# Moving small pieces of the first round between VectorE, ScalarE and GpSimd, and cutting v's projection in two

## The chip, the cores and the metric
One core of one Trainium2 chip runs the whole kernel. The metric is device time in microseconds, as the median of several executions.

## What is computed
A transformer block with a conditioning vector per sequence, then a conditioned layer norm. x has 64 sequences of 64 tokens of 256 features; there are 16 heads of 16 features, and a hidden layer of 1024.

```python
x = x + a_alpha * attention(gamma_a * rmsnorm(x) + beta_a)      # gamma, beta, alpha: t @ w.T, per sequence
x = x + f_alpha * (silu(h @ gate_w.T) * (h @ hidden_w.T) @ out_w.T + out_b)
#   with h = gamma_f * rmsnorm(x) + beta_f
y = (layernorm(x) * weight + bias + tanh(cond @ lin_w.T + lin_b)) * weight + bias
```

## The kernel before, in words
The 4096 tokens are cut into eight groups of eight sequences (512 tokens). Every stage of a group holds 128 partitions by 512 columns or a multiple. Products in full precision are made of three passes: each fp32 operand is split into a high part, which is the operand rounded to fp32r, and a low part, the rest; TensorE does high by high, low by high and high by low (`passes`). The weights are split this way too, once, during the first round: nine chunks are loaded through stage buffers (`stage`, chunks 0 to 8: wqk, wv, wo, four quarters of gh, two halves of wout), a rounding makes the high part (`cut_hi`) and a subtraction the low part (`cut_lo`).

The order of the work on each engine is written out by hand: each engine has its own queue of instructions, which waits on semaphores. In the loop the attention of group g runs interleaved with the feed-forward part of group g - 1. The first round (`first` on each engine) has no feed-forward part beside it: only the attention of group 0, the statistics, transposes and half a projection of k of group 1, and the preparation of the weights. Behind it `head(1)` projects v and q of group 1 around the transposes of the normed x2 (q's two halves stand before and behind them already), and `main(1)` begins with the first gate product of group 0 (L768).

The names that the change touches, in the order of the first round:

- `rsqrt_both(1)` on VectorE: the reciprocal roots of the second x's mean squares, eight small instructions on 128x8 (L1245 to L1270). GpSimd scales the second x with them (L1841), and TensorE transposes it (L495) as soon as k's second form (`par_k`, L999) has left the banks.
- `v_proj(0)`: 24 matmuls (L546), then the four `scores_for_max` (L582), whose maxima VectorE takes (`max_over_keys`, L1358); `transpose_max` (L593), `negate_max` (L1364), then the scores for the exponentials (`first_scores`, L617 and L605).
- `keep_v` (L1020) copies v out of its banks, two DMAs swap its halves of partitions, and `place_v_kept`, `place_v_swapped` (L1029, two instructions each) put it into `vblk`. `v_ready` counts the four.
- The attention of group 0 goes in four parts, `FIRST_ORDER` = (h 0, part 0), (h 1, part 0), (h 0, part 1), (h 1, part 1): exponentials (`first_exp`, L1068), sums (`first_sums`, L678), values (`first_values`, L692), `first_reciprocal` (L1393), `first_product` (L1405), and the split of the product (`first_o_split`, L1080 and L1746). The reciprocal of part 1 of a half is written over that of part 0 (`work_c[:, 0, quarter(h)]`), so it waits for the product.
- `o_proj(0)` (L701) with half of k's projection of group 1 (L511) between its pieces, then on VectorE `residual1_half` (L1424, L1426), `stats_x2`, `norm2` (L1443) and, behind TensorE's transposes, `gamma_x2` (L1454).
- Weight chunk 5 is rounded by VectorE (`CUT_ON_DVE`, L1410), all others by ScalarE (L968); all low parts are GpSimd's (L1826, and in halves L1832). They share the count `stage_lo`. Stage 8 uses the buffer of stage 5, so the DMA queue waits for the low part of chunk 5 before it loads it.

## Time and profile before

| | us |
|---|---|
| median of three executions | 488.96 |
| lowest and highest of them | 488.87, 489.3 |
| profiled execution | 488.55 |
| its span, first to last instruction | 486.8 |
| busy in the span: TensorE (matmuls) | 470.7 (97%) |
| VectorE | 373.3 (77%) |
| GpSimd | 273.7 (56%) |
| ScalarE | 241.9 (50%) |
| mean granted clock of TensorE, as a share of full speed | 0.995 |

The span is the time between the first and the last instruction in the trace; the profiled execution took somewhat longer than its span. A timeline gives the start and the duration of an instruction, or of several of one kind in a row (x4), in microseconds from the start of the span. Two instructions in a row on one engine often overlap by up to 0.1 us in the records, so the distance from one start to the next (the pitch) is a little less than the duration. What stands in square brackets at the end of a row is how long the engine had been idle and what it waited for. L12 is line 12 of the kernel.

### The profile page before, as it was taken

To read this page: it belongs to the slowest core of one execution; us is meant where nothing else is said; L and a number is where in the kernel's file an instruction comes from. 1 tells how busy PE (TensorE), PEld (TensorE's weight loads), DVE (VectorE), ACT (ScalarE), POOL (GpSimd) and SP (SyncE) were. 2 spreads that over 40 slices of the span, in tenths; PEclk is the share of its full clock that TensorE was granted. 3 is DMA by queue.
4 is the path that set the end of the run, shared out by engine and by line. 5 is a ranking of instruction groups with operands and counts; after the bars stand their busy time and mean duration, and the time that the engine had idled before them with its cause. 6 is when DMAs were issued, how large, how long until landed. Compare 5 with 4: busy or idle time off the path is not lost.

```text
span 486.8 us, 11925 instructions
## 1 busy us (share of the span) xinstructions
PE 470.7 (97%) x4547; PEld 399.6 (82%) x4547; DVE 373.3 (77%) x770; ACT 241.9 (50%) x373; POOL 273.7 (56%) x192
## 2 busy tenths in 40 slices
PE   7899999999999999999999999999999999999992
PEld 4678787998789888898879987898888978789992
DVE  5998875778876789579876788767895798684765
ACT  3885743355533756246453555437563476413341
POOL 3483655754385454844577543864548445626573
PEclk9999999999999999999999999999999999999997
DMA  7832295004540075301844045510745015500113
GB/s 196 301 89 86 53 252 113 3 2 134 129 128 25 1 197 119 93 0 29 230 65 86 0 123 136 125 26 0 200 90 119 0 23 152 131 2 4 41 48 83
DMA packets 36044, 44.23 MB, mean 91 GB/s; under 512 B 3120, under 2 KB 31024, under 8 KB 36016
## 3 DMA queue, kind: packets, MB, share of 16 engines
q1 hardware_dynamic: 36016, 43.85, 36.0%
q8 instruction: 18, 0.29, 0.3%
q14 instruction: 10, 0.08, 0.1%
HBM read 35.18 MB, written 4.47 MB: 81 GB/s over the span
## 4 chain that ended last, share of the span: by engine, by line
PE 86%; DVE 5%; ACT 3%; POOL 2%; issue 2%; DMA 1%; DVEq 0%; ACTq 0%; POOLq 0%
PE banks L768 32%; PE banks L786 17%; PE banks L511 7%; PE banks L617 6%; PE banks L701 5%; PE banks L546 4%; PE banks L807 3%; PE banks L660 3%; PE banks L665 3%; PE banks L605 2%; PE banks L738 1%; PE banks L582 1%; DMA xtok<-x_in 1%; PE banks L468 1%; PE banks L823 1%
## 5 line engine op out<-in xcount | busy, mean ns | idle before, releaser
L768 PE MATMUL banks<-x2s,gh 128*128 128x512 f32 x672 | 167.5, 397 | 0.7 <-ACT x2s L1089 0.5
L768 PEld LDWEIGHTS banks<-x2s,gh 128*128 128x128 f32 x672 | 122.7, 188 | 28.1 <-issue 0.9
L1791 POOL TENSOR_TENSOR hs<-act_t,hs 128x512 fp32r<-128x512 f32 x56 | 72.1, 1287 | 124.9 <-ACT hs L1051 94.2
L786 PE MATMUL banks<-wout,hs 128*128 128x256 f32 x672 | 91.7, 286 | 0.4 <-POOL hs L1791 0.4
L786 PEld LDWEIGHTS banks<-wout,hs 128*128 128x128 f32 x672 | 85.3, 188 | 5.3 <-POOL hs L1791 0.7
L1051 ACT ACTIVATE hs<-act_t 128x512 fp32r<-128x512 f32 x56 | 35.3, 631 | 70.6 <-DVE act_t L1465 70.6
L1044 ACT ACTIVATE act_t<-banks 128x512 f32<-128x512 f32 x56 | 33.5, 599 | 68.9 <-PE banks L768 68.4
L1461 DVE SCALAR_TENSOR_TENSOR act_t<-act_t,banks 128x512 f32<-128x512 f32 x56 | 38.4, 686 | 31.4 <-ACT act_t L1044 30.9
L1375 DVE RECIPROCAL work_c<-banks 128x512 f32<-128x512 f32 x14 | 47.0, 3356 | 3.3 <-PE banks L660 3.3
L511 PE MATMUL banks<-xs,wqk 128*128 128x512 f32 x192 | 47.7, 394 | 0.7 <-ACT xs L979 0.7
L1465 DVE SCALAR_TENSOR_TENSOR act_t<-act_t,banks 128x512 f32<-128x512 f32 x56 | 38.5, 688 | 5.0 <-PE banks L768 1.5
L511 PEld LDWEIGHTS banks<-xs,wqk 128*128 128x128 f32 x192 | 34.7, 188 | 7.9 <-ACT xs L979 1.0
L1358 DVE TENSOR_REDUCE smax<-banks 128x16 bf16<-128x1024 f32 x32 | 37.5, 1218 | 3.8 <-PE banks L582 3.8
L1068 ACT ACTIVATE pt<-banks 128x1024 f32<-128x1024 f32 x30 | 29.1, 1020 | 8.5 <-PE banks L617 8.1
L617 PE MATMUL banks<-qpair,kpar 64*128 64x128 f32 x512 | 32.7, 276 | 0.4 <-DVE negmax L1364 0.4
L617 PEld LDWEIGHTS banks<-qpair,kpar 64*128 64x128 f32 x512 | 30.1, 188 | 1.4 <-issue 1.4
L993 ACT ACTIVATE kpair<-banks,cst 128x1024 bf16<-128x1024 f32 x16 | 17.0, 1112 | 20.6 <-PE banks L511 20.6
L546 PE MATMUL banks<-wv,xs 128*128 128x256 f32 x192 | 26.2, 287 | 0.1
L546 PEld LDWEIGHTS banks<-wv,xs 128*128 128x128 f32 x192 | 24.4, 191 | 1.8 <-DVE x L1426 0.5
L701 PE MATMUL banks<-wo,os 128*128 128x256 f32 x192 | 25.0, 284 | 0.3 <-ACT os L1080 0.3
L807 PE MATMUL banks<-x2s,gh 128*128 128x256 f32 x192 | 25.1, 282 | 0.0
L1739 POOL TENSOR_TENSOR os<-work_c,os 128x512 fp32r<-128x512 f32 x14 | 18.1, 1294 | 11.7 <-ACT os L1074 11.7
(158 smaller groups left out, 751.0 us busy)
## 6 DMA issues: line engine op xcount, KB each, us to landing
xtok<-x_in SPq DMA_DIRECT2D x8, 512.0 KB, 5.3
xres<-x_in SPq DMA_DIRECT2D x8, 512.0 KB, 7.2
work_c<-xn SPq DMA_DIRECT2D x16, 256.0 KB, 3.6
row_aa<-rows_dram SPq DMA_DIRECT2D x16, 256.0 KB, 6.6
row_af<-rows_dram SPq DMA_DIRECT2D x16, 256.0 KB, 7.5
row_b<-rows_dram SPq DMA_DIRECT2D x16, 256.0 KB, 6.2
shift<-rows_dram SPq DMA_DIRECT2D x16, 256.0 KB, 6.1
y<-final SPq DMA_DIRECT2D x7, 512.0 KB, 3.2
```

What stands on the lines that cost most here:

```text
L511: last = mm(banks[:, base + m, :], wqk[:, a, k, c:c + P], xs[:, b, k, :], start=(n == 0), stop=(n == 5))
L546: last = mm(banks[:, base + t // 2, D * (t % 2):D * (t % 2) + D], xs[:, a, k, P * t:P * t + P], wv[:, b, k, :], start=(n == 0), stop=(n == 5))
L617: last = mm(score_region(base, i, half), kpar[r, h, b], qpair[r, h, :, L * b:L * b + L], start=start and i == 0, stop=not start and i == 3)
L701: last = mm(banks[:, bank_of_proj(g) + t // 2, D * (t % 2):D * (t % 2) + D], os_[:, b, k, P * t:P * t + P], wo[:, a, k, :], start=(n == 0 ...
L768: last = mm(banks[:, base + part, :], gh[:, a, k, w:w + P], x2s[:, b, k, :], start=(n == 0), stop=(n == 5))
L786: last = mm(banks[:, t // 2, D * (t % 2):D * (t % 2) + D], hs[:, c % 2, b, P * t:P * t + P], wout[:, a, c, :], start=(c == 0 and a == b an ...
L807: last = mm(banks[:, base + part, 0:HALF], gh[:, a, k, w:w + P], x2s[:, b, k, HALF * half:HALF * half + HALF], start=(i == 0), stop=(i == 5))
L1358: V.tensor_reduce(smax[:, :, 8 * n:8 * n + 8], banks[:, base:base + 2, :].rearrange("p a (x c) -> p a x c", c=L), AX.X, ALU.max).then_inc( ...
L1375: V.reciprocal(work_c[:, 0, :], banks[:, den_bank, :]).then_inc(o_steps, 1)
L1461: V.scalar_tensor_tensor(out=a, in0=a, scalar=1.0, in1=banks[:, base, :], op0=ALU.add, op1=ALU.mult).then_inc(h_steps, 1)
L1465: V.scalar_tensor_tensor(out=a, in0=a, scalar=0.5, in1=banks[:, base + 1, :], op0=ALU.mult, op1=ALU.mult).then_inc(h_steps, 1)
L1791: tt(hs[:, c % 2, 1, :], act_t[:, c % 2, :], hs[:, c % 2, 0, :].bitcast(F32), ALU.subtract)\
```

## The change
It touches the first round alone.

- Of the second x's roots, VectorE does the first four of eight instructions. [...]
- v's projection of group 0 is cut into two halves of 12 matmuls; the first scores for the maxima go between them. The signal that v is there comes after the second half.
- ScalarE splits q ahead of rounding chunk 2, rounds chunk 3 behind the placement of v's kept half, and does the second instruction of `place_v_swapped` behind the second exponential.
- Chunk 4 is rounded by GpSimd, which does `finish_shift` ahead of it and the low parts of chunks 3 and 4 behind. Chunk 5 is rounded by ScalarE, and its low part is VectorE's, behind the norm of x2. The counts (`stage_hi`, `stage_lo`) are renumbered, and stage 8's load waits for the new one.
- The reciprocals of part 1 get places of their own in `x2n`. VectorE does three reciprocals, two products, a reciprocal and two products, where it did two, two, two and two. TensorE does the sums of the third part ahead of the values of the first.
- The first half of chunk 6's low part on GpSimd waits for the first half's statistics of x2 and no longer for the normed x2.

```diff
-CUT_ON_DVE = (5,)
+HI_ON_POOL, LO_ON_DVE = 4, 5
...
 # sync
                 if n == 8:
-                    sp.wait_ge(stage_lo, 6)
+                    sp.wait_ge(stage_lo_dve, 1)
...
 # tensor
+            def project_v_half(h):
+                if h == 0:
+                    pe.wait_ge(stage_hi, 2)
+                    pe.wait_ge(stage_lo, 2)
+                return project_tiles(bank_of_v(0), (2 * h, 2 * h + 1))
...
                 k_proj(0)
                 q_proj(0)
-                v_proj(0)
+                project_v_half(0)
                 scores_for_max(0, 0)
+                project_v_half(1).then_inc(v_mm, 1)
                 scores_for_max(0, 1)
...
                 first_scores(3)
+                first_sums(2)
                 first_values(0)
                 first_values(1)
-                first_sums(2)
                 first_sums(3)
...
 # scalar
                 pair_k(0, range(2))
+                pair_q(0)
                 cut_hi(2)
-                cut_hi(3)
-                pair_q(0)
                 keep_v(0)
                 par_k(0)
                 act.wait_ge(zeroed, ZEROED)
                 place_v_kept(0)
-                cut_hi(4)
-                place_v_swapped(0)
+                cut_hi(3)
+                place_v_swapped(0, (0,))
                 first_exp(0)
                 first_exp(1)
+                place_v_swapped(0, (1,))
                 first_exp(2)
                 xs_split(1)
                 first_exp(3)
                 first_o_split(0)
                 first_o_split(1)
-                cut_hi(6)
+                cut_hi(5)
                 first_o_split(2)
                 first_o_split(3)
+                cut_hi(6)
...
 # vector
+            def first_recip(m):
+
+                h, part = FIRST_ORDER[m]
+                return x2n[:, h, :] if part else work_c[:, 0, quarter(h)]
...
                 if part:
-                    dve.wait_ge(o_steps, h + 1)
                     dve.wait_ge(den_mm, h + 1)
...
+            def cut_lo(n):
+                dve.wait_ge(stage_hi, hi_count(n))
+                V.tensor_tensor(chunks[n][2], stage_view(n), chunks[n][1].bitcast(F32), ALU.subtract)\
+                    .then_inc(stage_lo_dve, 1)
...
-                rsqrt_both(1)
+                v, y, t = roots_of_both
+                rsqrt_seed(norm1_steps, RS, v, y)
+                V.tensor_tensor(t, y, y, ALU.mult).then_inc(norm1_steps, 1)
+                dve.wait_ge(norm1_steps, RS + 2)
+                V.tensor_tensor(t, t, v, ALU.mult).then_inc(norm1_steps, 1)
+                dve.wait_ge(norm1_steps, RS + 3)
+                V.scalar_tensor_tensor(out=t, in0=t, scalar=-10.0 / 3.0, in1=t, op0=ALU.add, op1=ALU.mult)\
+                    .then_inc(norm1_steps, 1)
                 q_out(0)
...
-                for n in CUT_ON_DVE:
-                    cut_hi(n)
-                for part in range(2):
-                    for h in range(2):
-                        first_reciprocal(2 * part + h)
-                    for h in range(2):
-                        first_product(2 * part + h)
+                first_reciprocal(0)
+                first_reciprocal(1)
+                first_reciprocal(2)
+                first_product(0)
+                first_product(1)
+                first_reciprocal(3)
+                first_product(2)
+                first_product(3)
...
                 norm2(0)
+                cut_lo(LO_ON_DVE)
                 gamma_x2(0)
...
 # gpsimd
+            def finish_roots():
+
+                v, y, t = roots_of_both
+                f = 3.0 / 8.0
+                ts = nc.gpsimd.tensor_scalar
+                pool.wait_ge(norm1_steps, RS + 4)
+                ts(t, t, 5.0, None, ALU.add).then_inc(root_steps, 1)
+                pool.wait_ge(root_steps, 1)
+                tt(y, t, y, ALU.mult).then_inc(root_steps, 1)
+                pool.wait_ge(root_steps, 2)
+                tt(t, y, y, ALU.mult).then_inc(root_steps, 1)
+                pool.wait_ge(root_steps, 3)
+                tt(t, t, v, ALU.mult).then_inc(root_steps, 1)
+                pool.wait_ge(root_steps, 4)
+                ts(t, t, -0.5 * f * f * f, 1.5 * f, ALU.mult, ALU.add).then_inc(root_steps, 1)
+                pool.wait_ge(root_steps, 5)
+                tt(y, t, y, ALU.mult).then_inc(norm1_steps, RS - 4)
...
                 cut_lo(1)
+                finish_roots()
                 pool.wait_ge(norm1_steps, RS * 2)
...
                 cut_lo(2)
+                finish_shift()
+                pool.wait_ge(ld_stage[HI_ON_POOL], 16)
+                nc.gpsimd.tensor_copy(chunks[HI_ON_POOL][1], stage_view(HI_ON_POOL)).then_inc(stage_hi_pool, 1)
                 cut_lo(3)
-                finish_shift()
                 cut_lo(4)
-                cut_lo(5)
                 xs_split(1)
                 for m in range(4):
                     first_o_split(m)
-                pool.wait_ge(x2n_scaled, TT)
+                pool.wait_ge(x2_stats, 2)
                 cut_lo_half(6, 0).then_inc(stage_lo, 1)
```

## Rows read from the trace of the kernel before

**Rows 1.** Busy time by stretch: busy us (instructions) per engine, clock, DMA.
```profile
65.00:475.00 410.00, 409.77 (x3971) 353.43 (x3972) 313.00 (x631) 198.49 (x313) 233.53 (x160) 1.00 0.34 81
480.00:486.80 6.80, 0.00 (x0) 0.00 (x0) 3.35 (x16) 0.00 (x0) 1.26 (x1) 0.64 0.23 78
```

**Rows 2.** TensorE's waits, 51 to 475 us: us in total, times, longest.
```profile
PE banks L786 <- POOL hs L1791: 0.4, 1, 0.4
```

**Rows 3.** Timeline, 12 to 30 us: start us, duration us, engine, line, operation.
```profile
13.44 5.54 PE L511 MATMUL banks<-xs,wqk 128*128 128x512 f32 x23 [0.69 <-ACT xs L979]
...
18.74 0.17 DVE L1255 SCALAR_TENSOR_TENSOR nt<-nt 128x8 f32<-128x8 f32 x1
18.82 3.03 PE L546 MATMUL banks<-wv,xs 128*128 128x256 f32 x24
...
19.75 2.74 DVE L1352 TENSOR_SCALAR qpar<-banks,cst 128x512 bf16<-128x512 f32 x4
...
19.79 1.90 POOL L1841 TENSOR_TENSOR xtok<-xtok,nt 128x1024 f32<-128x1024 f32 x1 [4.30 <-DVE nt L1270]
...
22.35 1.03 ACT L1020 ACTIVATE xn<-banks 128x1024 f32<-128x1024 f32 x1
22.41 4.61 DVE L1358 TENSOR_REDUCE smax<-banks 128x16 bf16<-128x1024 f32 x4
...
25.18 0.73 POOL L1772 TENSOR_TENSOR shift<-shift,final 64x256 f32<-64x256 f32 x1
...
25.53 1.07 PE L495 MATMUL banks<-cst,xtok 128*128 128x128 f32 x8 [0.32 <-ACT kpar L999]
...
27.07 0.21 PE L593 MATMUL banks<-identb,smax 64*32 64x64 bf16 x4
...
27.71 1.28 ACT L1029 ACTIVATE vblk<-work_c 64x512 f32<-64x512 f32 x2
```

**Rows 4.** Timeline, 28 to 43 us.
```profile
29.15 2.20 ACT L1068 ACTIVATE pt<-banks 128x1024 f32<-128x1024 f32 x2 [0.15 <-PE banks L605]
...
30.44 0.68 DVE L1410 CAST gh<-x2c 128x1024 fp32r<-128x1024 f32 x1
...
31.04 3.53 DVE L1393 RECIPROCAL work_c<-banks 128x256 f32<-128x256 f32 x2
...
34.78 0.87 DVE L1405 TENSOR_TENSOR work_c<-banks,work_c 128x256 f32<-128x256 f32 x2 [0.21 <-PE banks L692]
...
35.66 3.37 DVE L1393 RECIPROCAL work_c<-banks 128x256 f32<-128x256 f32 x2
35.77 0.63 PE L692 MATMUL banks<-x,vblk 128*32 128x64 f32 x32
...
36.78 1.22 PE L701 MATMUL banks<-wo,os 128*128 128x256 f32 x8
...
39.55 0.69 DVE L1424 TENSOR_TENSOR banks<-banks,row_aa 128x512 f32<-128x512 f32 x1
...
40.14 1.92 PE L701 MATMUL banks<-wo,os 128*128 128x256 f32 x12 [0.28 <-ACT os L1080]
...
42.09 0.70 DVE L1424 TENSOR_TENSOR banks<-banks,row_aa 128x512 f32<-128x512 f32 x1 [0.19 <-PE banks L701]
```

**Rows 5.** Timeline, 41 to 66 us.
```profile
46.16 1.14 DVE L1443 TENSOR_SCALAR x2n<-x,nt 128x256 f32<-128x256 f32 x4
...
47.38 1.28 POOL L1832 TENSOR_TENSOR gh<-row_af,gh 128x512 fp32r<-128x512 f32 x1 [6.12 <-DVE x2n L1443]
...
48.18 1.29 DVE L1454 TENSOR_TENSOR x2g<-banks,tabs 128x512 f32<-128x512 f32 x2 [0.88 <-PE banks L738]
...
49.51 1.04 DVE L1448 TENSOR_TENSOR x2g<-x2g,tabs 128x512 f32<-128x512 f32 x1
...
50.81 3.50 PE L768 MATMUL banks<-x2s,gh 128*128 128x512 f32 x12 [0.50 <-ACT x2s L1089]
...
60.07 1.04 ACT L968 ACTIVATE wout<-x2c 128x1024 fp32r<-128x1024 f32 x1
```

More of the change, by code:

```diff
@@ L193, in build @@
             sem, ("den_first", "o_first", "recip_first", "o_hi_first", "o_lo_first"))
-        stage_hi_dve, stage_lo_rest = sem("stage_hi_dve"), sem("stage_lo_rest")
+        stage_hi_pool, stage_lo_dve, stage_lo_rest = sem("stage_hi_pool"), sem("stage_lo_dve"), sem("stage_lo_rest")
+        root_steps = sem("root_steps")
         last_dve, last_pool = sem("last_dve"), sem("last_pool")
@@ L313, in build, with hi_count @@
         block = ctx.enter_context(nc.Block())
+        roots_of_both = [nt1[:, i].rearrange("p a t -> p (a t)") for i in range(3)]
+        def hi_count(n):
+            return n if n > HI_ON_POOL else n + 1
         @block.sync
@@ L420, in step @@
                 if first:
-                    sp.wait_ge(stage_lo, 8)
+                    sp.wait_ge(stage_lo, 7)
                     load_b(0)
@@ L533, in v_proj @@
                 base = bank_of_v(g)
-                if not later(g):
-                    pe.wait_ge(stage_hi, 2)
-                    pe.wait_ge(stage_lo, 2)
-                elif not isinstance(g, int) or g > 1:
+                if not isinstance(g, int) or g > 1:
                     pe.wait_ge(h_steps, 2 * CH * (g - 1))
@@ L540, in v_proj, with project_tiles @@
                     pe.wait_ge(x2_steps, X2)
-                project_v(base, range(V_EARLY if later(g) else TT))
+                project_v(base, range(V_EARLY))
+            def project_v_half(h):
[3 more added lines that the diff above has]
+                return project_tiles(bank_of_v(0), (2 * h, 2 * h + 1))
             def project_v(base, tiles):
+                project_tiles(base, tiles).then_inc(v_mm, 1)
+            def project_tiles(base, tiles):
                 for t in tiles:
@@ L547, in project_v @@
                                   xs[:, a, k, P * t:P * t + P], wv[:, b, k, :], start=(n == 0), stop=(n == 5))
-                last.then_inc(v_mm, 1)
+                return last
             def v_rest(g):
@@ L747, in gate_hidden @@
                     if not later(f):
-                        pe.wait_ge(stage_lo, EARLY + 4)
+                        pe.wait_ge(stage_lo, EARLY + 3)
+                        pe.wait_ge(stage_lo_dve, 1)
                     if not alternate:
@@ L779, in ffn_out @@
                 if not later(f) and c % (CH // 2) == 0:
-                    pe.wait_ge(stage_lo, EARLY + 5 + c // (CH // 2))
+                    pe.wait_ge(stage_lo, EARLY + 4 + c // (CH // 2))
                 pe.wait_ge(h_hi, CH * f + c + 1)
@@ L1021, in keep_v, with place_v @@
                                      ACT.Copy).then_inc(v_out, 1)
-            def place_v(g, src, same):
+            def place_v(g, src, same, es):
                 by_tile = vblk[:, :, :, :, :].rearrange("p (t s) j e d -> p t s j e d", s=2)
                 v = src.rearrange("p (t j e d) -> p t j e d", t=TT, e=2, d=DH)
-                for e in range(2):
+                for e in es:
                     r = slice(64 * e, 64 * e + 64)
@@ L1033, in place_v_kept, with place_v_swapped @@
                 act.wait_ge(v_out, 2 * g + 1)
-                place_v(g, v_kept, True)
-            def place_v_swapped(g):
+                place_v(g, v_kept, True, range(2))
+            def place_v_swapped(g, es=range(2)):
                 act.wait_ge(v_moved, 32 * g + 32)
-                place_v(g, v_swapped, False)
+                place_v(g, v_swapped, False, es)
             def tanh(f, c, base=2):
@@ L1392, in first_reciprocal @@
                     dve.wait_ge(den_first, h + 1)
-                V.reciprocal(work_c[:, 0, quarter(h)], banks[:, FIRST_DEN[h], quarter(part)]).then_inc(recip_first, 1)
+                V.reciprocal(first_recip(m), banks[:, FIRST_DEN[h], quarter(part)]).then_inc(recip_first, 1)
             def first_product(m):
@@ L1763, in keep_x2 @@
                 else:
-                    pool.wait_ge(stage_lo, len(chunks))
+                    pool.wait_ge(stage_lo, len(chunks) - 1)
                 pool.wait_ge(ld_b, 32 * f + 32)
```

13 lines of the change are left out of this document (5 added, 8 removed).

## The prediction, made before the changed kernel had run

> **What bounds the kernel now.** I read first the table of busy time by stretch. From 65 to 475 us TensorE is busy 409.77 of 410 us [rows 1]: behind the first round nothing can be won or lost but the moment at which that stretch begins. So the question is by how much the first round (about 12 to 65 us) gets shorter or longer. The waits of TensorE between 51 and 475 us show that even behind the first gate product (50.81 us) there is only one of note, 0.4 us for a low part of the hidden layer [rows 2]; that wait hangs on work that starts after the gate product and moves with it. So the start of the first gate product is the gauge: its shift is the change's worth, one for one. Then I read the timeline of the three stretches ahead of it, [rows 3] (queries to transposed maxima), [rows 4] (attention of group 0 and its projection) and [rows 5] (norm and gate), and walked the new order of each queue through the durations of the old one.
>
> **The front, 18 to 28 us.** VectorE's roots lose four instructions: it has done the fourth by 18.91 (18.74 + 0.17) instead of the eighth at 19.72. The queries are projected at 18.98 (13.44 + 5.54), so VectorE's split of q starts at about 19.02 instead of 19.75, 0.72 us sooner, and the four maxima (22.41 to 27.02) end at about 26.3 [rows 3]. That gain does not get through whole. ScalarE copies v when all of it is projected: the 24 matmuls have a pitch of 0.12 us ((3.03 - 0.28) / 23), the first 12 run 18.82 to 20.26; then the first scores stand in the queue, waiting for half of q's split (19.02 + half of 2.74 = 20.4) and taking some 0.3 (eight small matmuls, where four took 0.21); then 12 matmuls, the last one ending at 20.75 + 11 x 0.12 + 0.28 = 22.35. ScalarE's copy began at 22.35 before, so it is no earlier, rather 0.05 later (its weight rounding, moved behind the split of q, fits into the wait). Behind it lie, unchanged, k's second form and TensorE's transposes of the second x, which need it: 25.58, plus 0.8 (1.07 less the 0.27 of the last one), plus two warm-up matmuls of 0.23 each ((5.54 - 0.39) / 22) is 26.85. Before, the transposes of the maxima started at 27.07, held by the maxima. So they start 0.2 us sooner, not 0.72 [rows 3]. **Term: -0.2.** Bounds: 0 if the copy of v slips further, -0.7 if the whole gain gets through.
>
> GpSimd takes six small instructions. The trace has no 128x8 one on it. The nearest row is 64x256 in 0.73 us, with 0.08 between dependent ones [rows 3]: at most 6 x 0.81 = 4.9 us; below, the 0.17 of VectorE's 128x8 rows with its 0.03 between them, 1.2 us. I take 0.3 each, 1.8, since the tile is small. Then the scaling of x (1.90) ends at 18.95 + 1.8 + 1.9 = 22.6, three microseconds ahead of the transposes; at the upper bound 25.75, 0.15 too late. Price 0, upper bound +0.15.
> The rounding of weight chunk 4 goes to GpSimd as a copy of 128x1024: below, half of the two-operand 1.90, above 2 x 1.28 (a two-operand 128x512) [rows 3, 5]; I take 1.9, as in the row with a broadcast. It must be over before chunk 3's low part, and that before the third exponential at 32.0. In my walk chunk 3's low part ends at 30.4, 1.6 us of cover; with both upper bounds at about 34, and the third exponential is 1.9 late, of which the reciprocals behind it feel 0.3. Price 0, upper bound +0.3. In a sentence of its own: the Trainium skill (GPSIMD Engine Reference, section 4.1) says that GpSimd takes a one-input pass at roughly line rate, and two-input ones at half VectorE's speed; by it the copy would be near 1 us and the sum the same.
>
> **The reciprocals, 28 to 43 us.** VectorE loses a rounding of 0.68 us at 30.44. But its first reciprocal also waits for all four placements of v, and the change puts the last one (half of 1.28) behind the second exponential. The exponentials run 29.15 to 31.35, now 0.2 sooner, so the placement ends 0.6 behind 31.15, and the first reciprocal starts at 31.75 instead of 31.04: +0.71, more than the rounding that left [rows 3, 4]. From there: a reciprocal has a pitch of 1.67 (two in 3.37, overlapping a little), three in a row end their turn at 36.76; the first two products take 0.3 each, the fourth reciprocal 1.67, two more products 0.6. VectorE is done at 39.7, before 39.55 to 39.64: the gaps that it saves (the first two took 3.53, and 0.21 of waiting stood ahead of the products) pay back what the late start cost.
> TensorE doesn't come out even. Its third values product waits for the first product of VectorE, which ran at 34.78 and now stands behind the third reciprocal at 36.76, done 37.18. Values to projection took 36.78 - 35.77 = 1.01: the projection starts at 38.22, not 36.78, +1.44. Up to the first half's end it does 12 matmuls of 0.13 ((1.22 - 0.28) / 7) and four of k's of 0.23, 2.5 in all, so VectorE gets the first half at about 40.85, the last one landed. It spends 2.35 on one half (39.55 to 41.90, where it sat 0.19 us until 42.09), or 2.2 without GpSimd beside it, so it is ready for the second at 43.1; TensorE, at 38.22 + 2.5 + 0.46 (two of k's) + 1.6 (12 of 0.13) = 42.8, has landed its last one (0.15) at 42.95. Before, that step was at 42.09 [rows 4]. **Term: +1.0** (this already holds the front's -0.2). Bounds: +0.7 (TensorE's path alone, 42.95 - 42.09 = 0.86, less 0.15) and +1.5 (TensorE's 1.44 kept whole).
>
> The other moves here cost nothing: chunk 5's rounding on ScalarE (1.04, between its splits of the output) lies in the 1.4 us in which ScalarE waits for the fourth reciprocal; chunk 6's low part starts earlier on an idle GpSimd.
>
> **The norm, 43 to 51 us.** From the second half's step to the gate everything is one chain, so it moves along. Behind the norm VectorE now takes chunk 5's low part, 128x1024. The nearest rows are 128x512 in 0.69 and 0.43 for half of that (0.87 for two): 0.26 us more for 256 columns, so 0.69 + 0.53 = 1.22, pitch about 1.15. Before, VectorE sat idle for 0.88 us there, ahead of 48.18. The cover is 0.96 us long (47.22 to 48.18), so +0.2 [rows 4, 5]. Bounds: 0 (0.9 us) and +0.9 (1.85).
> The upper one is a rule weighed against a row: VectorE's shift of x2 (128x512, both operands in SBUF) took 1.04 us while GpSimd did its own, 0.69 to 0.70 being usual for that shape [rows 4, 5]. The Trainium skill (GPSIMD Engine Reference, section 1) has this as contention for shared SBUF interfaces when VectorE has two SBUF inputs; the trace agrees, and by it the piece would cost 1.85. I take 1.22, since GpSimd's neighbour, the half chunk at 47.38, has been moved to about 43.2 and is over.
> The last stage load of the DMA queue now waits for this piece and is issued at about 49.5 instead of 37.35. Its rounding stood at 60.07, over 10 us behind: hidden, by the two gate products. Without that cover it would cost its landing time. The move of v behind it in the same queue is needed only at 56 us. **Term: +0.2.**
>
> **Sum.** +1.0 + 0.2 = +1.2 us at the first gate product, 52.0 instead of 50.81, and the same at the end. The profiled execution took 488.55 us (span 486.8, 1.75 around it), 0.4 under the median of the three runs, 488.96; the shift is added to the median: 490.2 us.
>
> **Rivals.**
> *The savings come through (faster).* VectorE is relieved of 0.8 us of roots, 0.68 of rounding and about 0.3 of gaps. If it were the only bound from 19 to 43 us, the gate would start 1.7 us sooner: 487.3 us. For it: VectorE is never idle between 20 and 27 us. It decides once the first reciprocal starts by about 30.0; against it stand the late placement and the products behind the third reciprocal, which TensorE waits for.
> *It evens out (same).* The front gains more (up to 0.7) or VectorE's half step is shorter, and the low part fits in its cover: +1.2 - 0.5 - 0.2 = +0.5, 489.5 us. For it: many of my margins are 0.1 to 0.2 us. Against: the 1.44 of the values' wait is large against all of them.
> *TensorE's clock falls.* The new gap between the last sums (about 35.6) and the third values (37.2) is 1.6 us long. The table shows clock 1.00 (2.4 GHz) up to 475 us, and 0.64 as a mean of the last 6.8 us, in which TensorE does nothing [rows 1]. If the clock falls to 1.2 GHz here, the 4 us of matmuls up to the half step take twice as long: about +4 more, 494 us. Against: nothing shorter than the end's idleness has brought it down.
> *GpSimd is dear.* Both upper bounds: +1.2 + 0.15 + 0.3 = +1.65, 490.6 us.
>
> **Chances.** A median can be told from the old one beyond 0.2%, 0.98 us. Forecast (+1.0 to +2.0): 0.50. GpSimd dear: 0.05. Clock or another large loss: 0.05. Evens out: 0.32. Faster: 0.08. So slower 0.60, same 0.32, faster 0.08. The range must reach into the even case and up to the upper bounds together (+1.0 + 0.5 + 0.7 + 0.15): 488.8 to 491.3. The likeliest case alone: 489.9 to 491.
>
> **What would show it.** In the profile of the changed kernel: maxima over by 26.3 but their transposes at 26.85; the first reciprocal at 31.75, released by ScalarE's placement of v; TensorE idle 1.6 us ahead of the third values, released by VectorE's first product at 37.2; VectorE's step for the second half at 43.1; the low part on VectorE, 1.22 us, ending just past the transposes of x2; the gate at 52.0; TensorE busy without gaps from 66 us on. The prediction is wrong if the transposes of the maxima come by 26.4, if the reciprocal starts before 31.2, or if the low part takes over 1.5 us.

## The result and the profile after

The changed kernel takes 491.07 us (median of 22 executions, 490.31 to 494.57) where the kernel before, on the same chip, takes 489.01 (22 executions, 488.4 to 492.63). The ratio is 1.0039, with an interval of 1.0025 to 1.0053: slower by less than half a percent, inside the range of the prediction (488.8 to 491.3) and 0.9 above the predicted time of 490.2. In both kernels the times fall into clusters, because in some executions TensorE's clock drops for a few microseconds; what follows keeps the executions with and without such a drop apart.

| | predicted | after |
|---|---|---|
| median | 490.2 | 491.07 |
| profiled execution, its span | | 492.97, 491.0 |
| maxima end | 26.3 | 26.22 |
| their transposes start | 26.85 | 27.94 |
| first reciprocal | 31.75 | 34.90 |
| third values | 37.2 | 40.21 |
| first gate product | 52.0 | 55.02 |

The busy time of TensorE on the page of the profile after: engine, busy us, share of the span, number of instructions, and the same for the other engines.

```profile
PE 473.1 (96%) x4547; PEld 402.1 (82%) x4547; DVE 371.3 (76%) x766; ACT 242.0 (49%) x373; POOL 273.4 (56%) x198
```

The table of busy time by stretch of the profile after answers to [rows 1].

```profile
65.00:475.00 410.00, 409.32 (x3955) 352.24 (x3954) 312.23 (x624) 197.91 (x310) 234.91 (x159) 1.00 0.33 83
```

TensorE is busy 409.32 of 410 us. The 0.45 less than before is the one wait of [rows 2] (0.4 us, L799 now), which has moved past 65 us with everything else: nothing has changed behind the first round, and the gauge of the prediction holds. The gate product starts 4.21 us later than in [rows 5], and the span is 4.2 longer than before (491.0 against 486.8). But 4.2 us is far more than the 1.2 that I summed, and more than the medians are apart. The windows of TensorE alone say where the rest is (window, its length, busy time and instructions, granted clock, DMA share and GB/s).

```profile
25.00:25.50 0.50, 0.00 (x0) 1.00 0.88 172
25.50:26.00 0.50, 0.43 (x4) 0.96 0.89 156
26.00:32.50 6.50, 6.05 (x51) 0.50 0.42 120
...
33.00:65.00 32.00, 29.66 (x366) 1.00 0.19 54
```

From 26 to 32.5 us the granted clock is 0.50, which is 1.2 GHz; on both sides it is 1.00 (2.4 GHz). The fall comes 0.4 us into the transposes of the second x; ahead of these TensorE had been idle for 1.04 us, since the last scores for the maxima. It is not the gap that my rival spoke of (1.16 us, ahead of the third values): after that one, the clock stays at 1.00. Two rows of the list of TensorE's waits, 12 to 65 us, name both gaps (us in total, times, longest):

```profile
PE banks L704 <- DVE work_c L1424: 1.2, 1, 1.2
PE banks L501 <- ACT kpar L1013: 1.0, 1, 1.0
```

The timeline after, 18 to 31 us, answers to [rows 3] (start us, duration us, engine, line, operation, idle time before):

```profile
18.67 1.59 PE L558 MATMUL banks<-wv,xs 128*128 128x256 f32 x12
18.78 0.25 POOL L1863 TENSOR_SCALAR nt<-nt 128x8 f32<-128x8 f32 x1 [3.43 <-DVE nt L1588]
...
20.31 0.20 POOL L1873 TENSOR_TENSOR nt<-nt 128x8 f32<-128x8 f32 x1
...
20.67 1.69 PE L558 MATMUL banks<-wv,xs 128*128 128x256 f32 x12
...
21.52 4.70 DVE L1373 TENSOR_REDUCE smax<-banks 128x16 bf16<-128x1024 f32 x4
...
22.39 1.02 ACT L1034 ACTIVATE xn<-banks 128x1024 f32<-128x1024 f32 x1 [0.29 <-PE banks L558]
...
25.57 1.58 PE L501 MATMUL banks<-cst,xtok 128*128 128x128 f32 x8 [1.04 <-ACT kpar L1013]
25.94 1.03 POOL L1894 CAST gh<-act_t 128x1024 fp32r<-128x1024 f32 x1
...
27.94 0.24 PE L605 MATMUL banks<-identb,smax 64*32 64x64 bf16 x4
...
28.63 2.08 PE L629 MATMUL banks<-qpair,kpar 64*128 64x128 f32 x16 [0.45 <-issue]
```

The signs of the prediction are there: GpSimd does the six root steps from 18.78 to 20.51 (I had put 1.8 us), the maxima are over at 26.22, chunk 4's copy takes 1.03 us. The low clock is seen in the durations: the transposes take 1.58 us, 1.07 in [rows 3], and the first 16 score matmuls 2.08. The timeline after, 32 to 52 us, answers to [rows 4] and, from 51 us, to [rows 5]:

```profile
34.24 0.63 ACT L1043 ACTIVATE vblk<-work_c 64x512 f32<-64x512 f32 x1
...
34.90 3.37 DVE L1412 RECIPROCAL work_c<-banks 128x256 f32<-128x256 f32 x2 [3.71 <-ACT vblk L1043]
...
38.19 1.69 DVE L1412 RECIPROCAL x2n<-banks 128x256 f32<-128x256 f32 x1
...
39.80 0.69 DVE L1424 TENSOR_TENSOR work_c<-banks,work_c 128x256 f32<-128x256 f32 x2
...
40.21 0.65 PE L704 MATMUL banks<-x,vblk 128*32 128x64 f32 x32 [1.16 <-DVE work_c L1424]
...
41.24 1.23 PE L713 MATMUL banks<-wo,os 128*128 128x256 f32 x8
...
46.17 0.69 DVE L1444 TENSOR_TENSOR banks<-banks,row_aa 128x512 f32<-128x512 f32 x1
...
51.28 1.22 DVE L1429 TENSOR_TENSOR gh<-x2c,gh 128x1024 fp32r<-128x1024 f32 x1
51.29 1.04 PE L750 MATMUL banks<-cst,x2n 128*128 128x128 f32 x8
```

The first reciprocal is released by ScalarE's placement of v (34.24 + 0.63), as I had it. Counted from it, the steps are those of the prediction: VectorE's first product 4.90 us behind, the third values 5.31 (predicted 5.45), the projection 6.34 (6.47), the second half's step 11.27 (11.35). Two rows of the same view, 52 to 64 us:

```profile
52.52 0.37 SPq L326 DMA_DIRECT2D x2c<-outT_in  x1
...
55.02 3.49 PE L781 MATMUL banks<-x2s,gh 128*128 128x512 f32 x12 [0.65 <-ACT x2s L1103]
```

VectorE's low part takes 1.22 us, as summed, and ends 0.17 us past the transposes of x2 (51.29 + 1.04). The load of stage 8 is issued at 52.52; its rounding runs at 64.28, still well covered.

So two things have to be told apart: what the new order costs, and what the fall of the clock costs, and whether the change brings it about.

### The profile page after: what moved, and what is told of

The parts are those of the page before. It is cut to its first block, busy times and chain, and to the rows that moved or that the text cites. A ratio compares the mean times of both kernels' runs of the same rounds, so it can differ in the third digit from the quotient of the medians.

```text
span 491.0 us, 11926 instructions
## 1 busy us (share of the span) xinstructions
PE 473.1 (96%) x4547; PEld 402.1 (82%) x4547; DVE 371.3 (76%) x766; ACT 242.0 (49%) x373; POOL 273.4 (56%) x198
## 4 chain that ended last, share of the span: by engine, by line
PE 85%; DVE 8%; ACT 2%; issue 2%; POOL 1%; DMA 1%; DVEq 0%; ACTq 0%
PE banks L781 31%; PE banks L799 17%; PE banks L517 8%; PE banks L629 6%; PE banks L713 4%; PE banks L558 4%; PE banks L672 3%; PE banks L820 3%; PE banks L677 3%; PE banks L617 2%; PE banks L594 1%; PE banks L750 1%; PE banks L836 1%; DMA xtok<-x_in 1%; DVE act_t L1507 1%
## 5 line engine op out<-in xcount | busy, mean ns | idle before, releaser
L799 PE MATMUL banks<-wout,hs 128*128 128x256 f32 x672 | 91.7, 286 | 0.4 <-POOL hs L1820 0.4
L799 PEld LDWEIGHTS banks<-wout,hs 128*128 128x128 f32 x672 | 85.3, 188 | 5.3 <-POOL hs L1820 0.7
L1481 DVE SCALAR_TENSOR_TENSOR act_t<-act_t,banks 128x512 f32<-128x512 f32 x56 | 38.4, 686 | 33.0 <-ACT act_t L1058 32.5
L629 PE MATMUL banks<-qpair,kpar 64*128 64x128 f32 x512 | 34.5, 286 | 0.4 <-issue 0.4
L629 PEld LDWEIGHTS banks<-qpair,kpar 64*128 64x128 f32 x512 | 31.7, 197 | 1.4 <-issue 1.4
```

Source lines behind the costliest of these rows:

```text
L629: last = mm(score_region(base, i, half), kpar[r, h, b], qpair[r, h, :, L * b:L * b + L], start=start and i == 0, stop=not start and i == 3)
L799: last = mm(banks[:, t // 2, D * (t % 2):D * (t % 2) + D], hs[:, c % 2, b, P * t:P * t + P], wout[:, a, c, :], start=(c == 0 and a == b an ...
L1481: V.scalar_tensor_tensor(out=a, in0=a, scalar=1.0, in1=banks[:, base, :], op0=ALU.add, op1=ALU.mult).then_inc(h_steps, 1)
```

## The experiments

Each was run twelve times, in five rounds against the kernel before. None leaves out or changes a part of what is computed; idle matmuls write where nothing is read. As the clock differs from one execution of the same kernel to the next, two numbers are given for each: the median of all twelve, with its ratio, and the median of those whose mean granted clock is 0.993 or more ("at full clock"). For the kernel before, that is 488.96 (21 of 35 executions, beside the first four kernels), 489.00 (16 of 35, beside the next four) and 488.85 (13 of 29, beside the last three); for the changed kernel 490.45 (11 of 22). In these two kernels the times leave a gap between the two sorts (489.25 to 489.85, and 490.83 to 491.32). In the others 0.992 can mean either, since the mean also holds the idle end, in which the clock is low in every profile: e4's and e9's profiled executions have 0.992 and no fall before 475 us. Inside one profile I read the distance from the first score matmul (the first L617 row of before, L629 of after) to the first gate product, where the clock is 1.00 in all the profiles read so (but for the first 0.1 us of e7's). Before, that is 50.81 - 27.72 = 23.09 us; the row of the kernel before is

```profile
27.72 0.49 PE L617 MATMUL banks<-qpair,kpar 64*128 64x128 f32 x4 [0.45 <-DVE negmax L1364]
```

**e1: the changed kernel with four more idle matmuls** in the gap ahead of the second x's transposes.

```diff
                 scores_for_max(0, 3)
+                warm_up(wqk[:, 0, 0], 4, 7)
                 transpose_x(1)
```

> The changed kernel with four more idle matmuls of 128x512 between the last scores for the maxima and the transposes of the second x, where TensorE sat idle for 1.04 us. Theory (the gap brings the clock down): the clock stays at 1.00 from 12 to 475 us in every run, the times lie together within 0.5 us near 490.4 to 490.6, and the gate product starts at 52.0 to 52.6. Rival (the clock falls for another reason, the small scores or the DMA traffic): some runs keep a mean clock of 0.991 or less and times of 491.3 and more.

Measured: 490.91 us, ratio 1.0021 [0.9995, 1.0047]; at full clock 490.74 (8 of 12). The clock has fallen in 4 of 12. I had expected it to stay up in every execution; that is a miss. Against the 11 of 22 without the idle matmuls, 4 of 12 doesn't show that they help, nor that they don't. But its profiled execution ran at clock 1.00 from 18 to 65 us, so it shows what the order alone costs (timeline, 18 to 54 us):

```profile
18.70 1.59 PE L558 MATMUL banks<-wv,xs 128*128 128x256 f32 x12
...
25.61 1.06 PE L501 MATMUL banks<-cst,xtok 128*128 128x128 f32 x8
...
26.42 0.71 PE L474 MATMUL banks<-wqk 128*128 128x512 f32 x2
...
27.07 0.21 PE L605 MATMUL banks<-identb,smax 64*32 64x64 bf16 x4
...
27.72 1.16 PE L629 MATMUL banks<-qpair,kpar 64*128 64x128 f32 x16 [0.44 <-issue]
...
32.02 3.37 DVE L1413 RECIPROCAL work_c<-banks 128x256 f32<-128x256 f32 x2 [1.41 <-ACT vblk L1044]
...
37.33 0.65 PE L704 MATMUL banks<-x,vblk 128*32 128x64 f32 x32 [1.16 <-DVE work_c L1425]
...
38.36 1.21 PE L713 MATMUL banks<-wo,os 128*128 128x256 f32 x8
...
43.28 0.69 DVE L1445 TENSOR_TENSOR banks<-banks,row_aa 128x512 f32<-128x512 f32 x1
```
```profile
52.14 2.11 PE L781 MATMUL banks<-x2s,gh 128*128 128x512 f32 x7 [0.65 <-ACT x2s L1104]
```

The gate is at 52.14, where I had predicted 52.0. From the first score matmul it is 24.42 us, against 23.09 before. The gate of after stood at 55.02: the 2.9 us between them are the low clock.

**e2: v projected whole**, the rest as in the changed kernel.

```diff
                 project_v_half(0)
-                scores_for_max(0, 0)
                 project_v_half(1).then_inc(v_mm, 1)
+                scores_for_max(0, 0)
                 scores_for_max(0, 1)
```

> The changed kernel with v projected whole again, ahead of the first scores. Theory: v's copy is ready 0.45 us sooner, k's second form and the transposes too, TensorE has no gap of 1 us ahead of them and keeps its clock; the gate product starts 0.1 to 0.3 us sooner than in the changed kernel at full clock (about 52.2), time 490.2. Rival (the halves are worth their 0.7 us of earlier maxima): the gate starts 0.3 us or more later than that, 490.8 and more.

Measured: 490.16 us, ratio 0.9998 [0.9971, 1.0026]; at full clock 490.06 (10 of 12), 0.4 under the changed kernel. In its profile the first score matmul comes 8.72 us behind the first of v's (28.11 - 19.39), in e1 9.02 (27.72 - 18.70), before 8.90. So with v whole the other moves at the front (roots on GpSimd, q split first) win 0.2 us, and the cut of v, which lets the maxima begin sooner, costs 0.3: it makes ScalarE's copy of v late (3.72 us behind the first matmul, 3.31 in e2), and k's second form and the transposes hang on that copy. In e9 below, which has the same moves and v whole, that distance is 8.87 (27.48 - 18.61), so the 0.2 is an upper figure. The clock fell in 2 of these 12.

**e3: the old order of reciprocals and sums.**

```diff
                 first_scores(3)
-                first_sums(2)
                 first_values(0)
                 first_values(1)
+                first_sums(2)
...
                 first_reciprocal(1)
-                first_reciprocal(2)
                 first_product(0)
                 first_product(1)
+                first_reciprocal(2)
                 first_reciprocal(3)
```

> The changed kernel with the old order of reciprocals and products (two, two, two, two) and of sums and values, the reciprocals of the second parts still in their own place. Theory (TensorE's values wait for a product that stands behind the third reciprocal): the projection starts 1.3 us sooner against the first reciprocal, the step for the second half 0.6 to 0.9 sooner, and runs at full clock take 489.6 to 489.9. Rival (VectorE alone is the bound, three in a row cost nothing): runs at full clock take 490.4 as before, within 0.2 us.

Measured: 490.72 us, ratio 1.0002 [0.9976, 1.0028]; at full clock 489.77 (5 of 12). From scores to gate it is 23.47 us (30.01 to 53.48): 0.95 less than in e1. The median of all twelve doesn't show it, as seven ran at a lower clock. From the first reciprocal to the projection it takes 4.98 us (34.31 to 39.29) where the changed kernel takes 6.34: 1.36 less, and 1.3 was expected.

**e4: v's swapped half placed whole, ahead of the exponentials.**

```diff
                 cut_hi(3)
-                place_v_swapped(0, (0,))
+                place_v_swapped(0)
                 first_exp(0)
                 first_exp(1)
-                place_v_swapped(0, (1,))
                 first_exp(2)
```

> The changed kernel with both placements of v's swapped half ahead of the first exponential, as before the change. Theory (the first reciprocal is held by the last placement): the first reciprocal starts 0.9 to 1.1 us sooner against the first scores, now released by the sums, and runs at full clock take 489.7 to 489.9, 0.5 to 0.7 less. Rival (the first exponential is pushed back by the placement and takes the gain back): 490.3 or more.

Measured: 491.37 us, ratio 1.0026 [0.9995, 1.0057]; at full clock 490.13 (4 of 12). Its timeline, 28 to 52 us:

```profile
28.04 1.16 PE L629 MATMUL banks<-qpair,kpar 64*128 64x128 f32 x16 [0.45 <-issue]
...
31.32 3.58 DVE L1411 RECIPROCAL work_c<-banks 128x256 f32<-128x256 f32 x2 [0.39 <-PE banks L690]
...
34.31 0.64 PE L690 MATMUL banks<-x,cst 128*32 128x256 f32 x8
...
35.02 1.76 DVE L1411 RECIPROCAL x2n<-banks 128x256 f32<-128x256 f32 x1
...
51.92 0.48 PE L781 MATMUL banks<-x2s,gh 128*128 128x512 f32 x1 [0.65 <-ACT x2s L1103]
```

The first reciprocal now waits for TensorE's sums and starts 3.28 us behind the scores, where it took 4.30 in e1 and 3.32 before. Of that one microsecond 0.54 reaches the gate (23.88 against 24.42). The rest is lost at the third reciprocal: it needs TensorE's third sums (34.31 + 0.64) and starts at 35.02, 3.70 us behind the first, where in e1 it starts 3.28 behind (35.30 - 32.02). By the times the gain is 0.32 (490.13 against 490.45), less than the 0.5 to 0.7 that I had expected, with four executions to go by.

**e5: all three edits of e2, e3 and e4.** What is left of the change: roots finished on GpSimd, q split first, chunk 4 rounded by GpSimd, chunk 5 by ScalarE, its low part on VectorE.

> The changed kernel with three of its parts undone: v whole, both placements ahead of the exponentials, and the old order of reciprocals, sums and values. What is left is the roots on GpSimd, the moved roundings and the low part on VectorE. Theory (these three parts are the loss, 0.4, 0.3 to 0.5 and 0.7 to 0.9 us, the low part behind the norm 0.14): at full clock 488.8 to 489.1, no slower than before the change. Rival (the moves of the roundings cost on their own): 489.4 or more at full clock.

Measured: 489.52 us, ratio 1.0002 [0.9975, 1.0028]; at full clock 489.08 (7 of 12), where the kernel before has 489.00. From scores to gate 23.17 us, 0.08 more than before. So the three edits hold all of the measured cost, and the moves that are left give nothing that can be measured: at most 0.2 us at the front, against the low part's 0.14.

**e6: as e5, and chunk 5's low part on GpSimd**, behind its splits of the output, with the counts renumbered.

```diff
                 norm2(0)
-                cut_lo(LO_ON_DVE)
                 gamma_x2(0)
...
                     first_o_split(m)
+                cut_lo(LO_ON_DVE)
                 pool.wait_ge(x2_stats, 2)
```

> As e5, and chunk 5's low part back on GpSimd, behind the splits of the first outputs. Theory (the low part outlasts its cover by 0.14): 0.14 us less than e5 at full clock, from the second half's step to the gate 8.72 instead of 8.86. Rival (GpSimd beside VectorE's statistics slows these by their shared interface, more than is won): as e5 or slower, the statistics over 0.5 us instead of 0.42.

Measured: 492.98 us, ratio 1.0063 [1.0034, 1.0091], the slowest here; not one of its twelve executions was at full clock, and the lowest was 491.65. Its timeline, 44 to 50 us:

```profile
44.99 0.50 DVE L1306 CUSTOM_DVE_ANT_0 x2n<-x 128x256 f32<-128x256 f32 x1
45.16 2.57 POOL L1852 TENSOR_TENSOR gh<-x2c,gh 128x1024 fp32r<-128x1024 f32 x1
...
45.42 2.60 DVE L1306 CUSTOM_DVE_ANT_0 x2n<-x 128x256 f32<-128x256 f32 x1
...
47.95 0.69 DVE L1442 TENSOR_TENSOR banks<-banks,row_aa 128x512 f32<-128x512 f32 x1
...
49.42 3.15 PE L558 MATMUL banks<-wv,xs 128*128 128x256 f32 x18 [2.02 <-DVE x L1444]
```

VectorE's second statistics of x2, 0.50 us for the one ahead of it, take 2.60 us. GpSimd's low part had started 0.26 us ahead of them and ends at 47.73; the statistics end 0.29 us later. The half steps wait behind them, and TensorE 2.02 us for those. The rival is right, and by far more than I had given it (over 0.5 us instead of 0.42). How much of the 492.98 is this wait and how much the clock, which was low in all twelve, isn't separated.

**e7: the kernel before with the new order of reciprocals alone** (three, two products, one, two products, places of their own, the third sums ahead of the values).

```diff
-                for part in range(2):
-                    for h in range(2):
-                        first_reciprocal(2 * part + h)
-                    for h in range(2):
-                        first_product(2 * part + h)
+                first_reciprocal(0)
+                first_reciprocal(1)
+                first_reciprocal(2)
+                first_product(0)
+                first_product(1)
+                first_reciprocal(3)
+                first_product(2)
+                first_product(3)
```

> The kernel before with one part of the change alone: three reciprocals in a row, in their own places, and the third sums ahead of the first values. Theory (TensorE's third values wait for a product that now stands behind the third reciprocal): the third values start 0.9 us later against the first scores, TensorE idle there, the gate 0.5 to 0.9 later, 489.5 to 489.9 at full clock. Rival (three in a row are free, or win the gaps of VectorE): 488.7 to 489.1.

Measured: 489.84 us, ratio 1.0006 [0.9984, 1.0028]; at full clock 489.70 (7 of 12), 0.7 over the kernel before. In its profile 23.75 us from scores to gate (29.82 to 53.57), 0.66 more, of which 0.05 is the tail of a low clock (the second 16 score matmuls come 1.24 us behind the first, 1.19 before). The order costs this much without the late placement. The same profile bears on the other question. Up to the sums this kernel is the one before, and its clock falls too, at the same place (windows of TensorE, as above):

```profile
26.00:27.00 1.00, 0.94 (x11) 0.76 0.60 135
27.00:28.00 1.00, 1.00 (x8) 0.50 0.97 209
```

So the clock can fall here without any part of the change.

**e8: the kernel before with a longer gap**: the two idle matmuls between the last scores for the maxima are taken out.

```diff
-WARM_LOADS, WARM_LAST_MAX, WARM_MAX, WARM_NORM = 3, 2, 2, 3
+WARM_LOADS, WARM_LAST_MAX, WARM_MAX, WARM_NORM = 3, 0, 2, 3
```

> The kernel before without the two idle matmuls ahead of the last scores for the maxima, so that TensorE stands idle there longer. If a gap at this place brings the clock down, more than the 14 in 35 runs of the kernel before have a mean clock under 0.993, and their times are 1 us and more above the rest. If the clock falls whatever the kernel does here, the share stays near 14 in 35, and the runs at full clock take 488.9 to 489.1.

Measured: 491.27 us, ratio 1.0026 [0.9999, 1.0053]. The clock was under 0.993 in 11 of 12, where it was in 19 of the 35 executions of the kernel before beside it; the one at full clock took 488.5. Its windows:

```profile
24.50:25.00 0.50, 0.01 (x2) 0.76 0.00 0
...
34.00:35.00 1.00, 1.00 (x11) 0.50 0.00 0
35.00:36.00 1.00, 1.00 (x20) 1.00 0.00 0
```

The fall comes between 24.5 and 25 us, inside a wait of 0.82 us ahead of the last scores (24.51 to 25.33), and the clock is back to 1.00 only at about 35. If both kernels fell equally often, a difference in share as large as this would come up in 3 of 100 such comparisons. So more idleness of TensorE at this place makes the fall more frequent, and the two idle matmuls that the kernel has there are worth their place.

**e9: the kernel before with the parts that had looked good**: roots finished on GpSimd, q split first, chunk 3 rounded behind the kept half of v, chunk 4 rounded by GpSimd. Chunk 5 is rounded by VectorE as before.

```diff
                 pair_k(0, range(2))
+                pair_q(0)
                 cut_hi(2)
-                cut_hi(3)
-                pair_q(0)
...
                 place_v_kept(0)
-                cut_hi(4)
+                cut_hi(3)
                 place_v_swapped(0)
...
                 cut_lo(2)
+                finish_shift()
+                pool.wait_ge(ld_stage[4], 16)
+                nc.gpsimd.tensor_copy(chunks[4][1], stage_view(4)).then_inc(stage_hi_pool, 1)
                 cut_lo(3)
-                finish_shift()
                 cut_lo(4)
```

> The kernel before with the parts of the change that the runs so far do not speak against: the second x's roots finished on GpSimd, q split ahead of the roundings of chunks 2 and 3, chunk 4 rounded by GpSimd; chunk 5 rounded by VectorE and its low part on GpSimd as before, v whole, both placements ahead of the exponentials, reciprocals in pairs. Theory: 0.14 us less than e5 at full clock for the low part and the front's 0.2 sooner start of the scores, 488.8 to 488.95 against 489.0 before, which a measurement cannot tell from it. Rival (the roots on GpSimd or the moved roundings cost something): 489.2 and more at full clock.

Measured: 490.07 us, ratio 1.0024 [1.0002, 1.0046]; at full clock 489.94 (6 of 12), 1.1 over the kernel before. I had expected a small gain; that is a miss, and the timeline, 29 to 36 us, shows why:

```profile
29.85 2.36 POOL L1837 TENSOR_TENSOR gh<-act_t,gh 128x1024 fp32r<-128x1024 f32 x1
...
30.28 2.48 DVE L1412 CAST gh<-x2c 128x1024 fp32r<-128x1024 f32 x1
...
32.68 3.36 DVE L1395 RECIPROCAL work_c<-banks 128x256 f32<-128x256 f32 x2
```

The rounding that took 0.68 us in [rows 4] takes 2.48 beside a low part of GpSimd (29.85 to 32.21), and the first reciprocal comes 5.20 us behind the scores (32.68 - 27.48) instead of 3.32. Of these 1.88 us 1.13 reach the gate (51.70 - 27.48 = 24.22, against 23.09).

**e10 and e11: e9, and the kernel before, with two more idle matmuls** (one between the last scores, one ahead of the transposes).

```diff
-WARM_LOADS, WARM_LAST_MAX, WARM_MAX, WARM_NORM = 3, 2, 2, 3
+WARM_LOADS, WARM_LAST_MAX, WARM_MAX, WARM_NORM = 3, 3, 2, 3
...
                 scores_for_max(0, 3)
+                warm_up(wqk[:, 0, 0], 1, 7)
                 transpose_x(1)
```

> e9 with two more idle matmuls in the stretch between v's copy and the transposes of the second x. If the idle time of TensorE in that stretch brings the clock down, fewer than the 33 in 70 runs of the kernel before lie under a mean clock of 0.993, and the median is 1 us below the kernel before's on the same chip; at full clock the time is e9's within 0.2 us. If the falls come from the earlier gaps (22 to 24 us) or are not to be steered, the share stays near a half.

> The kernel before with the same two idle matmuls and nothing else. Theory on the clock as for e10: fewer than 33 in 70 runs under 0.993, full-clock time 489.0 within 0.2 us. Rival: the share stays near a half.

Measured: e10 489.88 us, ratio 1.0003 [0.9982, 1.0024], full clock in 8 of 12 (489.69). e11 489.34 us, ratio 0.9995 [0.997, 1.0019], full clock in 6 of 12 (488.76). In e11 the share is that of the kernel before, and in e10 4 of 12 can't be told from a half; e10's median is 0.1 us below the kernel before's, where I had expected 1 us. So neither run shows that two more idle matmuls steer the clock. One pattern, seen only afterwards, is left: none of the 36 executions of e1, e10 and e11 has a mean clock of 0.986 or less, where 19 of the kernel before's 99 have. But none of the 24 of e3 and e7 has one either, and they have no more idle matmuls than the kernels they come from, so it isn't shown to be the idle matmuls' doing. No version here beats the kernel before: e5 and e11 equal it within what can be measured.

## Why the prediction was right, and where it was off

**The clock falls without the change too.** The changed kernel was under 0.993 in 11 of 22 executions, the kernel before in 14 of 35, 19 of 35 and 16 of 29, 49 of 99 together, and e7 shows the fall ahead of the first instruction that it moves. Whether the change makes it more frequent is open: in the comparison that gave the result, only 5 of the kernel before's 22 times are above the gap (489.92 and more; all others are 489.30 or less), against the changed kernel's 11 of 22. Chance gives a difference as large in 12 of 100 such comparisons. A profile with a fallen clock misleads: it puts the change at 4.2 us. At full clock it is 490.45 against about 488.95, +1.5 us or 0.3%; in that comparison alone, 490.45 against 488.87, the median of the other 17. That the medians of all executions lie 2.06 apart, and not 1.5, comes from that difference in share: the kernel before's median, 489.01, lies in its cluster of full clock, and the changed kernel's falls between two clusters (it has 490.3 to 490.8, 491.3 to 491.7 and 492.9 to 494.6).

**Part of the hit is luck.** The mechanisms and their sum (+1.2 predicted, +1.5 measured) hold for executions at full clock. The median of all of them stands at 491.07 only because exactly half have fallen: with one more of the 22 in a lower cluster it would be about 491.3, at the upper end of the range, and I had given the clock and any other large loss a chance of 0.05. My rival on the clock had about the right size (+4; the executions that fell took 0.9 to 4 us more) and the wrong place: I had looked at the new gap at 36 us, where nothing fell, and hadn't asked whether the clock was steady before the change. I had one profile of before, at 1.00, and three times within 0.4 us.

**Step by step, at full clock.** Distances in us, before from its rows, after from e1:

| step | before | predicted | e1 |
|---|---|---|---|
| v's first matmul to first scores | 8.90 | 8.70 | 9.02 |
| to first reciprocal | 3.32 | 4.23 | 4.30 |
| to third values | 4.73 | 5.45 | 5.31 |
| to projection | 1.01 | 1.02 | 1.03 |
| to the second half's step | 5.31 | 4.88 | 4.92 |
| to the gate product | 8.72 | 8.90 | 8.86 |
| sum | 31.99 | 33.18 | 33.44 |

- *Front, -0.2 predicted, +0.12 measured: the mis-sized term.* The maxima did end early, and that gain did not get through, as I said. But the copy of v slipped by 0.19, not by 0.05 (v's second half began 2.00 us behind the first and took 1.69, where I had 1.93 and 1.60). And from the transposes of x to those of the maxima it took 1.46 us (25.61 to 27.07), where I had 0.8 + 0.46: the two idle matmuls between them took 0.65, as the 25.53 to 27.07 before was nearly all TensorE's own time and only 0.08 the maxima's. I had read it in [rows 3] as a hold by the maxima of 0.2 to 0.3. My bound of "0 if the copy of v slips further" was the right side, and still too low.
- *First reciprocal, +0.91 predicted, +0.98 measured*, by the placement of v, the mechanism that I named; e4 takes it away.
- *The order of the reciprocals.* The wait of the third values was 1.16 us in after, e1 and e2 (predicted 1.6), and it outweighs what VectorE saves: e7 puts the order alone at +0.6 to +0.7. That it pays back some 0.4 in the step from projection to half came as summed.
- *Low part on VectorE, +0.2 predicted, +0.14 measured*, with the 1.22 us that I had interpolated. The upper bound of 1.85 did not come, as GpSimd was done with its half chunk (46.33 + 1.28) before it.
- *GpSimd.* Roots 1.73 us (1.8), copy 1.03 (I took 1.9). The Trainium skill (GPSIMD Engine Reference, section 4.1) says roughly line rate for one input, and the trace agrees with it. Both were hidden and cost nothing.

One premise at the front was wrong besides. Before the change, ScalarE's copy of v didn't wait for the projection. That was over at 21.85 (18.82 + 3.03 in [rows 3]); the copy at 22.35 stood behind ScalarE's split of q, the last one landing at 22.46:

```profile
19.78 2.68 ACT L1010 ACTIVATE qpair<-banks,cst 128x512 f32<-128x512 f32 x4
```

So with the roots relieved and q split sooner a whole v is copied 0.2 us sooner (e2: 3.31 us behind the first matmul, 3.53 before), and cutting v gives that up as well.

"Savings come through" fell as foreseen: the reciprocal did not start by 30.0. "Evens out" asked for a larger gain at the front or a shorter half step, and a low part that fits its cover: the front lost 0.12, the half's step took 4.92 us where I had 4.88, and the low part outlasted its cover by 0.14. By times at full clock the three edits give 0.4 for v's cut, 0.7 for the order and 0.3 for the placement, together 1.4 of 1.5; these are medians of ten, five and four executions, and those five reach from 489.21 to 490.48, so that they add up so well is not to be leaned on. By distances inside the profiles the last two are 0.71 and 0.30 when undone one on the other (e4 to e5, e3 to e5), but 0.95 and 0.54 when each is undone alone: each makes the other dearer by about 0.24.

**What stays open.** Why the clock falls in one execution and not in the next, and whether the change raises the share. e8 shows that a longer gap makes the fall more frequent; e1, e10 and e11 don't show that a shorter one makes it rarer. I have no profile at full clock of e5, e7 or the kernel after itself; their order costs are read behind the fall, where the clock is 1.00 again.

## What to carry to other kernels

Before reading a shift of a microsecond or two from a pair of profiles, compare their granted clocks in the same stretch, and the mean clock of all executions: here about half of them, of either kernel, had lost 1 us or more, up to 5, to a fall in the first round. When a chain of two engines is reordered, ask for each product who waits for it: three reciprocals in a row kept VectorE busy, and made TensorE wait for the first product. And before work is put on an idle GpSimd, look at what VectorE does beside it: GpSimd's subtractions of two tiles in SBUF held VectorE's statistics (e6) and its rounding (e9) until they were over.

## What the runs showed that I had not expected

*VectorE waits for all of GpSimd's instruction.* In e6 0.42 us became 2.60, ending 0.29 after GpSimd's, in e9 0.68 became 2.48, ending 0.55 after it (32.76 against 32.21). I had read the 1.04 in [rows 5] as a slowing by half, and taken it to hold in proportion, which gave the bound of 1.85; it is a stop until the other is done. The row of [rows 5] says so itself, beside GpSimd's row of the same view:

```profile
48.96 1.04 POOL L1752 TENSOR_TENSOR x2g<-x2g,tabs 128x512 f32<-128x512 f32 x1 [0.29 <-DVE x2g L1454]
```

GpSimd's ends at 50.00, VectorE's at 50.55 (49.51 + 1.04). In all three cases VectorE's instruction ends behind GpSimd's by its own undisturbed length less 0.13 to 0.14 us: 0.29 of 0.42, 0.55 of 0.68, 0.55 of 0.69. The Trainium skill (SBUF — State Buffer, section "Who interferes with whom") states that whichever starts first holds the shared pair of ports for its whole instruction, and that VectorE contends when it has two SBUF inputs or is in a two-port mode. The runs agree that VectorE stops until GpSimd is done: the statistics read x as both of their inputs; the rounding has one input, and that it runs in a two-port mode is not shown here. This also gives the move of chunk 5's rounding to ScalarE a reason that I had not seen: e9 keeps that rounding on VectorE beside a busier GpSimd and loses 1.9 us at the first reciprocal.

*The clock falls in half of the executions of an unchanged kernel*, to 1.2 GHz, and at two places: between 12 and 18 us in the profiles of e3, e5, e6, e7 and e10, between 24.5 and 35 in those of after, e5, e6, e7, e8 and e11. Both stretches have waits of TensorE, but the fall need not come in one: in e8 it came inside a wait, in after 0.4 us behind the end of one (26.0 against 25.57), and in e7 at 26.5, 1.6 us behind the last wait of note (0.73 us, over at 24.86). In e6 it falls once more, at 50.8, 1.4 us behind the end of the new wait of 2.02 us (granted clock 0.70 from 50 to 52 us, 0.50 to 54).
